# The Delta mixer of a four-stage stack: both flights' exponentials in a row on ACT, then the SiLU of both

## The reference

```python
def _L0_attn_b_ref(hidden_states, ...):
    qkvz = hidden_states @ w_qkvz.T; ba = hidden_states @ w_ba.T
    yc = silu(causal_conv4(concat(q, k, v)))          # 8 key heads, 16 value heads, 128 wide
    q, k, v = split(yc)
    beta = sigmoid(b); g = -exp(A_log) * softplus(a + dt_bias)
    q, k = l2norm(q), l2norm(k)
    def step(S, xs):                                  # per token and value head
        S = S * exp(gt)
        delta = (vt - kt @ S) * bt
        S = S + outer(kt, delta)
        return S, (qt * scale) @ S
    o = scan(step, 0, ...)
    xf = o * silu(z)
    return (xf * rsqrt(mean(xf * xf)) * norm_weight) @ w_out.T
```

## Time and profile before

| | |
|---|---|
| median of three runs | 4134.11 us |
| the profiled execution | 4134.86 us, span 4133.0 us |
| TensorE matmuls | 3763.0 us busy, 91% of the span |
| TensorE weight loads | 2994.9 us, 72% |
| DVE | 2146.8 us, 52% |
| ACT | 1712.9 us, 41% |
| POOL | 500.8 us, 12% |
| mean granted clock of TensorE | 0.967 of full speed |

### The profile page before, as it was taken

The page is one execution under the profiler, slowest core; times in us unless marked ns, Lnnn a source line. Parts: engine busy times, 40 slices in busy tenths (PEclk is TensorE's granted clock), DMA queues, the critical chain, the costliest instruction groups (busy, mean ns, idle before and its releaser), DMA issues. The chain is left out here.

```text
span 4133.0 us, 57354 instructions
## 1 busy us (share of the span) xinstructions
PE 3763.0 (91%) x19926; PEld 2994.9 (72%) x19926; DVE 2146.8 (52%) x4713; ACT 1712.9 (41%) x4129; POOL 500.8 (12%) x344
## 2 busy tenths in 40 slices
PE   4847799999699999999999999999999999699998
PEld 2323478788478878788787887877878887488787
DVE  5547155555355454555545545455554554355554
ACT  3324222322255554554545545455454554323321
POOL 0102210200011010110101101111110110300200
PEclk8979899999799999999999999999999999899999
DMA  2010210211200000000000000000000000301210
GB/s 78 0 41 0 93 61 31 102 51 41 91 4 1 1 22 1 1 22 0 21 2 0 21 2 0 21 2 0 22 1 0 6 21 11 113 31 71 82 51 31
DMA packets 53735, 118.90 MB, mean 29 GB/s; under 512 B 2688, under 2 KB 3840, under 8 KB 52480
## 3 DMA queue, kind: packets, MB, share of 16 engines
q1 hardware_dynamic: 53504, 115.96, 8.0%
HBM read 90.78 MB, written 25.17 MB: 28 GB/s over the span
## 5 line engine op out<-in xcount | busy, mean ns | idle before, releaser
L1408 DVE COPY_PREDICATED b_Tt<-b_new_part,banks 128x256 f32<-128x256 uint8 x384 | 186.6, 486 | 816.8 <-PE banks L1644 816.8
L1587 PE MATMUL banks<-b_x_cur,b_w_cur 128*128 128x256 f32 x2048 | 517.7, 382 | 7.9 <-ACT b_w_cur L1062 7.1
L765 PE MATMUL banks<-f_x_hi,f_w_hi 128*128 128x512 f32 x1024 | 408.1, 399 | 39.5 <-ACT f_silu L634 22.6
L1155 ACT COPY b_em<-banks 128x256 f32<-128x256 f32 x384 | 144.4, 376 | 688.4 <-PE banks L1636 688.4
L1644 PEld LDWEIGHTS banks<-b_Tt,b_em 128*128 128x128 f32 x3072 | 399.9, 192 | 22.0 <-ACT b_em L1155 2.2
L1636 PE MATMUL banks<-b_T,b_At 128*128 128x128 f32 x3072 | 411.4, 277 | 0.5 <-ACT b_T L1149 0.5
L1644 PE MATMUL banks<-b_Tt,b_em 128*128 128x128 f32 x3072 | 406.7, 275 | 1.3 <-ACT b_em L1155 1.0
L765 PE MATMUL banks<-f_x_lo,f_w_hi 128*128 128x512 f32 x1024 | 405.6, 396 | 0.0
L765 PE MATMUL banks<-f_x_hi,f_w_lo 128*128 128x512 f32 x1024 | 405.5, 396 | 0.0
L1587 PEld LDWEIGHTS banks<-b_x_cur,b_w_cur 128*128 128x128 f32 x2048 | 357.3, 192 | 41.0 <-issue 8.4
L1636 PEld LDWEIGHTS banks<-b_T,b_At 128*128 128x128 f32 x3072 | 377.6, 192 | 9.2 <-ACT b_T L1147 6.7
(11 more groups left out here) (241 smaller groups left out, 6372.7 us busy)
## 6 DMA issues: line engine op xcount, KB each, us to landing
f_x_tok<-rows SPq DMA_DIRECT2D x16, 1024.0 KB, 7.5
b_w_load<-in_b_qkvz SPq DMA_DIRECT2D x8, 1536.0 KB, 8.0
f_stage<-in_ffn_gate SPq DMA_DIRECT2D x8, 1024.0 KB, 6.9
f_stage<-in_ffn_up SPq DMA_DIRECT2D x8, 1024.0 KB, 7.5
f_stage<-in_ffn_down SPq DMA_DIRECT2D x8, 1024.0 KB, 4.9
f_x_res<-rows SPq DMA_DIRECT2D x8, 1024.0 KB, 5.6
f_part<-f_x_res SPq DMA_DIRECT2D x8, 1024.0 KB, 4.3
f_x_res<-f_part SPq DMA_DIRECT2D x8, 1024.0 KB, 5.5
```

The source lines that it names most:

```text
L765: mm = pe.matmul(bank, w[:, b, kind, cols], x[:, k, :], start=(k == 0 and i == 0), stop=(k == KD - 1 and i == 2))
L1155: act.copy(half(f.X, i + 1, 0), half(f.wide, i + 1, 0)).then_inc(f.s["X"], 1)
L1408: dve.copy_predicated(half(f.Tt, i + 1, 1), new_part[:, i, :].rearrange("p (a n) -> p a n", n=LEVELS[i + 1]), half(f.right, i + 1, 1)).the ...
L1587: mm = pe.matmul(bank[i][:, 2 * part:2 * part + 2, :], w_cur[:, k, col:col + P], f.x_cur[:, k, :, :], start=(k == 0), stop=(k == KD - 1))
```

## The change

In the list of steps of a pair, on three engines:

- ACT: `decay(B, m)` stands ahead of `silu_qkv(B, m)` and `silu_z(B, m)`, no longer behind them. So a pair has the exponentials of A and B one after the other, and then B's SiLU and, in its last third, the next A's.
- DVE: `log_decays(B, m, h, c)` is the pair's first step, no longer the third.
- TensorE: `decays(B, m)` stands ahead of `products(A, m)`, no longer behind it.

```diff
@@ ACT, pair @@
                 tokens(A, m)
+                decay(B, m)
                 silu_qkv(B, m)
                 silu_z(B, m)
-                decay(B, m)
                 values(A, m)
                 tokens(B, m)
@@ DVE, pair @@
                 m, c = h * PAIRS + mm, 2 * mm
+                log_decays(B, m, h, c)
                 factors(A, m, h, c)
                 key_scales(A, m)
-                log_decays(B, m, h, c)
                 scales(A, m)
@@ TensorE, pair @@
                 if not first:
                     project_out(B, m - 1)
+                decays(B, m)
                 products(A, m)
-                decays(B, m)
                 tokens(B, m)
                 qk(A, 1, ALL)
                 turn_back(A, m, 0)
```

## The result

The changed kernel takes 4203.84 us in the median of four runs (4195.87 to 4207.97), the kernel before, now with four runs, 4134.03 us (4128.75 to 4137.38): 1.0164 of the time, interval [1.0152, 1.0176]. Slower by 70 us, where 74 were forecast.

The account below looks back on a forecast made before the run. TensorE, busy 2176 of 2240 us in the mixer, was taken as the bound. Lateness of 47 us plus clock falls of 27 us made 74 us, from 4134 to 4208 us; range 4174 to 4240.

Parts of the forecast that it names:

- Loads removed: nothing.: ACT, before exp(B) and the next silu(A): 64 loads of 1.28 us go, none on TensorE's path, so no gain.
- The stall, 2.2 us, behind decays(B), exponential, load and SiLU.: TensorE before tokens(B): a new stall of 2.2 us a pair, waiting for ACT's later SiLU of B.
- Net 1.53 a pair.: TensorE from turn_back(A,0) to the pair's end: 1.53 us late after cover, 47 us over 31 pairs.
- Falls of the clock, 16 by 1.67.: TensorE behind the new stall: one in two brings half clock, 16 falls of 1.67 us, 27 us.
- Is DVE late next?: DVE's first T of A: 0.73 us later through gU of B, still 0.9 us ahead of the new turn_back.
- The last pair, 0.5.: Last pair, no projection between tokens(B) and turn_back: loses about 0.5 us, set against smaller losses at head ends.
- likely case: Whole kernel: about half the stalls before tokens(B) bring a clock fall, 4208 us; chance 0.53.
- few falls: Rival, behind the stall at tokens(B): the clock holds, up to four falls, 4181 to 4188 us; chance 0.18.
- nearly all: Rival, behind the stall at tokens(B): nearly every stall brings a clock fall, 4233 us; chance 0.13.

Follow-up runs that it names:

- early_decay: Changed kernel, with decays(B) ahead of B's out-projection on TensorE and gU of B made by DVE in the pair before; 4136.81 us, ratio 1.0004.
- act_undone: Changed kernel, with ACT's order as before the change, four table loads a pair, TensorE and DVE as changed; 4129.15 us, ratio 0.9992.
- copy_in_before: Kernel before the change, with a plain copy in place of both SiLUs, so no table loads in the pairs; 4122.27 us, ratio 0.9976.
- pe_undone: Changed kernel, with decays(B) behind products(A) on TensorE again, ACT and DVE as changed; 4259.57 us, ratio 1.0302.
- copy_in_after: Changed kernel, with a plain copy in place of both SiLUs, so no table loads in the pairs; 4127.56 us, ratio 0.9984.
- fill_two: Changed kernel, with two matmuls of no use put on TensorE in the stall before tokens(B); 4173.58 us, ratio 1.0095.
- dve_undone: Changed kernel, with log_decays(B) back in third place in DVE's pair, ACT and TensorE as changed; 4200.86 us, ratio 1.0163.

## Why the prediction was right

- *Loads removed: nothing.* Held. early_decay has two a pair and act_undone four, and the intervals of both hold 1. That a load was on the path was true of one that the change does not remove (copy_in_before); the prediction had looked at none but the two that go.
- *The stall, 2.2 us, behind decays(B), exponential, load and SiLU.* 2.28 measured, 32 times. Each link of the chain is in the fences above, and pe_undone, early_decay and copy_in_after move it by what they move the chain.
- *Net 1.53 a pair.* 1.40. Up to turn_back(A,0) the loss is 10.23 - 8.63 = 1.60 (1.58 forecast), and its restart gives 0.05 as forecast. Counted from the out-projection's start in the two pairs shown, TensorE is then still 1.53 late at the projection (L1587) ahead of the last turn_back(B) (2247.67 before, 2279.51 after), 1.44 at that turn_back (2248.63 and 2280.38) and 1.41 at the first solve(A) behind it (2249.99 and 2281.71). So the last 0.1 is given back around that one place, which I had at nothing. In dve_undone it is not given back, so DVE's move has to do with it; by which wait was not traced. 31 by 0.13 are 4 us, all that this term was too large by.
- *Falls of the clock, 16 by 1.67.* 16 more, by 1.67 to 1.7; fill_two shows the price apart from the stall. That it was just 16 is luck to a degree. The prediction's own count was eleven falls behind fourteen stalls, and one in two was a choice; and dve_undone, with the same 2.28 us stall, had 13 intervals with a fall where the changed kernel had 17.
- *Is DVE late next?* I had its T of A later by gU's 0.73. Counted from the out-projection's start it is 0.06 later: L1400 ends 8.57 us behind it before (2209.08) and 8.63 after (2239.45). DVE's chain did come late, L1397 starting 7.21 us behind that point instead of 6.61, but L1397 itself then took 0.55 less. First the kernel before and then the changed one (DVE and POOL in order of time):

```profile
2207.12 1.24 DVE L1397 TENSOR_TENSOR b_Tt<-b_At,b_joins 128x512 f32<-128x512 f32 x1
...
2206.54 1.27 POOL L1007 TENSOR_TENSOR b_em_i<-b_em,b_upto 128x512 f32<-128x512 f32 x1 [3.44 <-ACT b_em L1120]
```

```profile
2238.03 0.69 DVE L1397 TENSOR_TENSOR b_Tt<-b_At,b_joins 128x512 f32<-128x512 f32 x1
2238.76 0.69 DVE L1400 TENSOR_TENSOR b_Tt<-b_Tt,b_ident 128x512 f32<-128x512 f32 x1
...
2235.98 1.27 POOL L1007 TENSOR_TENSOR b_em_i<-b_em,b_upto 128x512 f32<-128x512 f32 x1 [1.97 <-ACT b_em L1120]
```

  With the exponential of B earlier against products(A), POOL's masking of it lies ahead of L1397, no more over it. Over the whole run, 17 of the 64 operations of L1397 took more than 0.9 us in the kernel before, each with a POOL operation running as it began; in the changed kernel none did, and none had POOL beside it. It changes no sum: turn_back came 1.6 us behind T (0.9 in the prediction), and with the 1.24 it would still have been 1.05, as an estimate. That POOL causes the 1.24 was not tested by itself.
- *The last pair, 0.5.* Its interval was 1.67 longer, with a longer stretch of half clock after (about 14 us against 10). How much of the 1.67 is the stall and how much the clock the runs do not settle.

The range's likely case held throughout; *few falls* and *nearly all* were the right neighbours, seen as fill_two (4173.58) and, with a longer stall, pe_undone.

The Trainium skill's "ScalarE: Activation LUTs", section "Table sets: the hidden batching unit", says to batch activations by table set. Here early_decay follows that rule and gains nothing that can be told, and the changed kernel shows what it costs if the regrouping puts a function behind a late producer. The Trainium skill's figure of some 2.66 us for a switch, in that page's section "What ACT_TABLE_LOAD costs", the traces don't bear out: the load starts 0.01 us after the exponential ends (2235.31 + 0.60 to 2235.92) and the SiLU 1.30 after that, and without the load the stall is 1.42 us shorter. (The excess that the prediction took from that figure as 1.35 us is 1.37, 2.66 less 1.29.)

## What to carry to other kernels

Count what an engine waits for on the bounding engine before you count its busy time: 82 us of loads were free where ACT stood idle behind them, and one of the loads left cost nearly the whole loss once a late producer stood in front of it. When instructions of one kind are brought together, the producer of the one that is pulled forward has to move further forward too, here past the out-projection. A new stall on TensorE may cost a fall of the clock beside its own length, here behind about half of those of 2.28 us; matmuls of no use in the gap got that part back, 30 of 70 us.

## What the hardware showed that I had not expected

- A stall of one length, 2.28 us, was followed by a fall in some intervals and not in others: 17 of 31 in the changed kernel, 13 of 31 in dve_undone. With 3.15 us it was 30 of 31. In the kernel before, where the longest in the pairs was 1.4, only the last pair, with its 2.09 us wait, had one; copy_in_after had one more, behind a stall of 2.39.
- The same 128x512 SBUF-to-SBUF multiplication on DVE took 1.24 us where a POOL multiplication ran beside it and 0.69 where none did; DVE's operations that read PSUM beside POOL's (L1383, L1393) kept their times, 0.68 and 1.11 us. The Trainium skill, "SBUF — State Buffer", section "SBUF: two separate sides", says that an operation of DVE with two inputs in SBUF and one of POOL that reads SBUF take the same port in turn, each for its whole length. The rows agree with it: DVE's operation ends 0.55 us behind POOL's (2208.36 and 2207.81), little less than the 0.69 that it takes alone.
- A 512-column fp32 matmul call is two recorded matmuls, 0.86 us together (2234.25 to 2235.11, one call of `decays`).
